# Causal attention layer of a decoder: float32r split products, reordered queues

## What is computed

```
h   = layernorm(x)                                # 16 batches of 128 rows x 256
qkv = h @ Wqkv.T                                  # 16 heads of 16
q   = q*cos + rotate_half(q)*sin ; k likewise
s   = einsum('bhqd,bhkd->bhqk', q, k) / 4 ; s[causal] = -inf
out = einsum('bhqk,bhkd->bhqd', softmax(s), v)
x   = x + out.reshape(...) @ Wout.T
```

## Time and profile before

| what | value |
|---|---|
| median of three runs | 1561.54 us (1561.36 to 1569.25) |
| the profiled execution, its span | 1564.6 us |
| TensorE busy | 1485.5 us, 95% |
| VectorE busy | 1068.3 us, 68% |
| ScalarE busy | 965.8 us, 62% |
| GpSimd busy | 727.0 us, 46% |
| mean granted TensorE clock | 0.983 |
| the causal block in it | from about 9 to 202 us |

### The profile page before, as it was taken

How to read it: one execution, slowest core, us unless ns; L and a number is a source line. 1 busy time by engine, 2 the same in 40 slices (tenths; PEclk the granted TensorE clock), 3 DMA queues, 4 the chain that set the end, 5 groups by cost and what they waited for, 6 DMA issues and landing times. The chain is left out here.

```text
span 1564.6 us, 30305 instructions
## 1 busy us (share of the span) xinstructions
PE 1485.5 (95%) x10256; PEld 1212.1 (77%) x10256; DVE 1068.3 (68%) x2475; ACT 965.8 (62%) x2612; POOL 727.0 (46%) x891
## 2 busy tenths in 40 slices
PE   5999979999999999899997999899999999989998
PEld 2666668888888888788874555489999999967887
DVE  4676657888888887655545777655566665588887
ACT  2667647777777777533325877577777777742222
POOL 3666625555555555233333433213444444447675
PEclk8999989999999999999997999999999999999999
DMA  6000020000000000000003000020000000000000
GB/s 246 2 1 1 2 97 5 3 5 3 5 3 4 3 3 2 22 1 1 1 5 130 2 2 1 15 92 8 8 8 8 1 8 5 1 1 14 11 15 17
DMA packets 15609, 29.82 MB, mean 19 GB/s; under 512 B 1505, under 2 KB 12002, under 8 KB 14690
## 3 DMA queue, kind: packets, MB, share of 16 engines
q1 hardware_dynamic: 15458, 27.89, 4.9%
HBM read 25.79 MB, written 2.10 MB: 18 GB/s over the span
## 5 line engine op out<-in xcount | busy, mean ns | idle before, releaser
L1453 POOL TENSOR_TENSOR weights_even<-weights_even,cross_reciprocal 128x512 f32<-128x512 f32 x64 | 66.6, 1041 | 201.9 <-DVE cross_reciprocal L1686 201.9
L934 POOL TENSOR_TENSOR cross_work<-cross_work,cross_reciprocal 128x512 f32<-128x512 f32 x64 | 66.6, 1040 | 174.6 <-DVE cross_reciprocal L1091 174.6
L1535 ACT ACTIVATE weights_even<-bank,cross_shift 128x128 f32<-128x128 f32 x256 | 90.5, 366 | 79.1 <-DVE cross_shift L1678 79.1
L1157 PE MATMUL bank<-ident,cross_work 128*128 128x128 f32 x768 | 117.6, 276 | 2.5 <-DVE cross_work L1069 2.2
L987 ACT ACTIVATE cross_work<-bank,cross_shift,cross_q_rms 128x128 f32<-128x128 f32 x256 | 113.6, 455 | 5.2 <-DVE cross_shift L1063 4.0
L1157 PEld LDWEIGHTS bank<-ident,cross_work 128*128 128x128 f32 x768 | 90.2, 141 | 30.0 <-DVE cross_work L1069 21.1
L2481 DVE TENSOR_REDUCE grouped_maxima<-bank 128x4 bf16<-128x512 f32 x128 | 82.3, 684 | 35.9 <-PE bank L2564 35.9
L1962 POOL TENSOR_TENSOR mlp_low_inner<-mlp_inner,mlp_high_inner 128x512 fp32r<-128x512 f32 x36 | 48.7, 1353 | 116.4 <-ACT mlp_high_inner L2005 116.4
L1676 DVE TENSOR_REDUCE cross_maxima<-bank 128x4 f32<-128x512 f32 x64 | 44.1, 690 | 84.6 <-PE bank L1818 84.6
L404 POOL TENSOR_TENSOR causal_masked_maxima<-causal_maxima,causal_constants 128x512 bf16<-128x512 bf16 x64 | 67.0, 1068 | 56.6 <-DVE causal_maxima L549 56.6
L2830 ACT ACTIVATE mx_silu<-bank 128x512 f32<-128x512 f32 x32 | 19.1, 598 | 113.4 <-PE bank L2980 113.3
(11 more groups left out here) (375 smaller groups left out, 5292.6 us busy)
## 6 DMA issues: line engine op xcount, KB each, us to landing
weights_even<-in_weights SPq DMA_DIRECT2D x2, 2560.0 KB, 11.8
weights_even<-in_weights SPq DMA_DIRECT2D x2, 1732.0 KB, 8.6
weights_odd_early<-in_weights SPq DMA_DIRECT2D x1, 3072.0 KB, 11.9
weights_odd_values<-in_weights SPq DMA_DIRECT2D x1, 3072.0 KB, 18.9
weights_odd_late<-in_weights SPq DMA_DIRECT2D x2, 1536.0 KB, 9.4
x<-in_x SPq DMA_DIRECT2D x4, 512.0 KB, 8.2
out<-mx_result SPq DMA_DIRECT2D x16, 128.0 KB, 1.7
weights_even<-in_weights SPq DMA_DIRECT2D x2, 512.0 KB, 5.8
```

The source lines that it names most:

```text
L934: pool.tensor_tensor(probs[x], probs[x], reciprocal[x][:, :].unsqueeze(2).to_broadcast([P, PER, P]), ALU.mult).then_inc(probs_divided, 1)
L1157: last = pe.transpose(bank[:, j * P:(j + 1) * P], source, core.ident[:, :])
L1453: pool.tensor_tensor(probs[x], probs[x], reciprocal[x][:, :].unsqueeze(2).to_broadcast([P, JOBS, P]), ALU.mult).then_inc(probs_divided, 1)
L1535: last = act.activation(probs[x][:, j, :], bank_scores[x][:, j * P:(j + 1) * P], ACT.Exp, scale=SCALE, bias=shift[x][:, j:j + 1], accum_ou ...
```

## The change

The four projections become three float32r products each. For that the block's own weights are split at its start, four pieces of 512 columns, by a ScalarE copy and a VectorE subtraction each. The two ScalarE copies of turned `h` and heads become one of up to 512 columns (`copy_turned`), followed by one VectorE subtraction of the same width (`low_turned`), which stands ahead of the maxima of pair 1; TensorE waits for it ahead of the value projection. The next block's weights are split by one ScalarE copy (`take_high`, last in the step) and one GpSimd subtraction a step later (`take_low`) in place of one VectorE and two GpSimd operations. On GpSimd the masked maxima of both pairs now stand ahead of that subtraction. VectorE normalises `h` one step earlier, behind the statistics, and takes the statistics of later chunks one step later. ScalarE's exponentials of pair 1 stand ahead of the mask of pair 1. TensorE subtracts the maxima of t pair 1 ahead of the scores of t+1 pair 0, those of t+1 pair 0 ahead of the scores of pair 1, and the transposed scores of pair 0 end the step that made them.

```
@@ scalar
+            act.wait_ge(core.weights_loaded[n], 16 * WEIGHT_PARTS)
+            for k in range(WEIGHT_JOBS):
+                columns = slice(512 * k, 512 * (k + 1))
+                act.activation(split[0][:, columns], raw[:, columns], ACT.Copy).then_inc(own_high, 1)
+            def copy_turned(t, s):
+                if batch_there(t + 2):
+                    act.wait_ge(layer.hT_filled, t + 3)
+                if batch_there(t - 2):
+                    act.wait_ge(headsT_filled, t - 1)
+                act.wait_ge(v_filled, min(nonneg(t + 1), BATCHES))
+                act.wait_ge(layer.y_filled, nonneg(t - 3))
+                act.activation(turned[s][0][:, turned_in(t)], bank_h[:, turned_in(t)], ACT.Copy)\
+                   .then_inc(turned_high, 1)
             def step(t, s):
-                    copy_hT(t + 2, s)
...
-                    copy_headsT(t - 2)
+                    copy_turned(t, s)
...
                     copy_keys_and_own_queries(t + 1, 1 - s)
+                if batch_there(t):
+                    exponentials(t, 1)
                 if batch_there(t + 1) and not begins(t + 1):
                     lay_mask(t + 1, 1)
                 if batch_there(t):
-                    exponentials(t, 1)
+                    take_high(t)
@@ vector
+            def low_turned(t, s):
+                dve.wait_ge(turned_high, turned_by(t))
+                dve.tensor_tensor(turned[s][1][:, turned_in(t)], bank_h[:, turned_in(t)],
+                                  turned[s][0][:, turned_in(t)].bitcast(F32), ALU.subtract).then_inc(turned_low, 1)
+            layer.dve_normalise(dve, 0)
+            for k in range(WEIGHT_JOBS):
+                dve.wait_ge(own_high, k + 1)
+                dve.tensor_tensor(split[1][:, columns], raw[:, columns], split[0][:, columns].bitcast(F32),
+                                  ALU.subtract).then_inc(own_low, 1)
             def step(t, s):
-                if batch_there(t + 2):
-                    layer.dve_normalise(dve, t + 2)
                 if batch_there(t + 1):
                     add_turned(t + 1)
+                if batch_there(t + 2) or batch_there(t - 2):
+                    low_turned(t, s)
                 if batch_there(t):
                     row_maxima(t, s, 1)
-                    take_high(t, s)
...
+                if batch_there(t + 3):
+                    if (t + 3) % CHUNK == 0:
+                        dve.wait_ge(chunk_statistics.rstd_ready, (t + 3) // CHUNK)
+                    layer.dve_normalise(dve, t + 3)
                 if batch_there(t + 2):
                     multiply_by_tables(t + 2)
@@ gpsimd
             def step(t, s):
                 if batch_there(t):
                     mask_maxima(t, s, 1)
-                if batch_there(t):
-                    split_weights(t, s)
                 if batch_there(t + 1):
                     mask_maxima(t + 1, 1 - s, 0)
+                if batch_there(t - 1):
+                    take_low(t - 1)
@@ tensor
+            def three_products(out, inputs, weights):
+                for c in range(EC):
+                    for x, y in PARTS:
+                        last = pe.matmul(out, inputs[x][:, c, :], weights[y][:, c, :],
+                                         start=(c == 0 and (x, y) == PARTS[0]),
+                                         stop=(c == EC - 1 and (x, y) == PARTS[-1]))
             def step(t, s):
-                if batch_there(t):
-                    scores_transposed(t, s, 0)
...
                     weigh_values(t - 1, 1 - s)
+                if batch_there(t + 2) or batch_there(t - 2):
+                    pe.wait_ge(turned_low, turned_by(t))
...
                     project_values(t + 1, 1 - s)
...
+                    project_heads(t - 2, s)
+                if batch_there(t):
+                    subtract_maxima(t, 1)
                 if batch_there(t + 1):
                     scores(t + 1, 1 - s, 0)
...
                 if batch_there(t + 1):
+                    subtract_maxima(t + 1, 0)
                     scores(t + 1, 1 - s, 1)
+                    scores_transposed(t + 1, 1 - s, 0)
```

More of the change, by code:

```diff
@@ L315, in place @@
             return part.rearrange(pattern, **sizes) if pattern else part
-        wqk = place(EC * 2 * EMBED, "p (c n) -> p c n", c=EC)
-        wv, wo = (place(EC * EMBED, "p (c n) -> p c n", c=EC) for k in range(2))
+        WEIGHT_JOBS = EC * 4 * EMBED // 512
+        raw = place(EC * 4 * EMBED)
+        split = [sbuf(f"{name}_weights", [P, EC * 4 * EMBED], F32R) for name in ("high", "low")]
+        wqk = [w[:, 0:EC * 2 * EMBED].rearrange("p (c n) -> p c n", c=EC) for w in split]
+        wv, wo = ([w[:, k * EC * EMBED:(k + 1) * EC * EMBED].rearrange("p (c n) -> p c n", c=EC) for w in split]
+                  for k in (2, 3))
         constants = sbuf("constants", [P, dram["causal_constants"].shape[1]])
@@ L325, in causal_attention @@
         qk_cos, qk_sin, qk = (place(2 * EMBED) for k in range(3))
-        hT = [layer.hT, place(EC * P, "p (c t) -> p c t", c=EC)]
+        turned = [[sbuf(f"{name}_turned{s}", [P, 2 * EMBED], F32R) for name in ("high", "low")] for s in range(2)]
+        hT = [[half[:, 0:EMBED].rearrange("p (c t) -> p c t", c=EC) for half in turned[s]] for s in range(2)]
+        headsT = [[half[:, EMBED:2 * EMBED].rearrange("p (c t) -> p c t", c=EC) for half in turned[s]]
+                  for s in range(2)]
         qT_bf = [sbuf(f"qT_bf{s}", [P, EC, P], BF16) for s in range(2)]
@@ L360, in chunk_at_end_of, with turned_in, turned_by @@
         def chunk_at_end_of(t):
-            return t + 3 if isinstance(t, int) and t + 3 in range(1, CHUNKS) else None
+            return t + 2 if t + 2 in range(1, CHUNKS) else None
         def begins(b):
             return isinstance(b, int) and b < 2
+        def turned_in(t):
+            return slice(0 if batch_there(t + 2) else EMBED, 2 * EMBED if batch_there(t - 2) else EMBED)
+        def turned_by(t):
+            return t + 3
         def slice_of(tensor, b):
@@ L432, in _ @@
         def _(act):
[L433 to L445, removed]
+            act.wait_ge(core.weights_loaded[n], 16 * WEIGHT_PARTS)
[11 more added lines that the diff above has]
+                   .then_inc(turned_high, 1)
+            qkT = bank_qkT.rearrange("p (x c t) -> p x c t", x=2, c=EC)
             def narrow_queries_and_own_keys(b, s):
@@ L671, in turn @@
                 last.then_inc(filled, 1)
-            def project_values(b, s):
-                pe.wait_ge(layer.hT_ready, b + 1)
-                for c in range(EC):
-                    last = pe.matmul(bank_h[:, 0:EMBED], hT[s][:, c, :], wv[:, c, :],
-                                     start=(c == 0), stop=(c == EC - 1))
-                last.then_inc(v_filled, 1)
-            def project_heads(b):
-                pe.wait_ge(headsT_ready, b + 1)
-                for c in range(EC):
-                    last = pe.matmul(bank_qk[:, 0:EMBED], headsT[:, c, :], wo[:, c, :],
-                                     start=(c == 0), stop=(c == EC - 1))
-                last.then_inc(layer.y_filled, 1)
+            def three_products(out, inputs, weights):
[4 more added lines that the diff above has]
+                                         stop=(c == EC - 1 and (x, y) == PARTS[-1]))
+                return last
@@ L687, in project_queries_and_keys, with project_heads @@
+            def project_values(b, s):
+                if b == 0:
+                    pe.wait_ge(own_low, WEIGHT_JOBS)
+                three_products(bank_h[:, 0:EMBED], hT[s], wv).then_inc(v_filled, 1)
+            def project_heads(b, s):
+                three_products(bank_qk[:, 0:EMBED], headsT[s], wo).then_inc(layer.y_filled, 1)
             def project_queries_and_keys(b, s):
-                pe.wait_ge(layer.hT_ready, b + 1)
+                pe.wait_ge(turned_low, turned_by(b - 2))
+                if b == 0:
+                    pe.wait_ge(own_low, WEIGHT_JOBS // 2)
@@ L689, in project_queries_and_keys @@
                 pe.wait_ge(qk_read, nonneg(b))
-                for c in range(EC):
-                    last = pe.matmul(bank_qk[:, :], hT[s][:, c, :], wqk[:, c, :], start=(c == 0), stop=(c == EC - 1))
-                last.then_inc(qk_filled, 1)
+                three_products(bank_qk[:, :], hT[s], wqk).then_inc(qk_filled, 1)
             def step(t, s):
-                if batch_there(t):
-                    scores_transposed(t, s, 0)
-                if batch_there(t):
-                    pe.wait_ge(v_ready, t + 1)
```

57 lines of the change are left out of this document (21 added, 36 removed).

## The result

The changed kernel takes **1571.48 us** (median of five runs, 1571.23 to 1576.34) against 1561.54: ratio 1.0052, 95% interval 1.0029 to 1.0076. Measured once more beside the experiments, twelve runs against 23 of the kernel before, it is 1570.52 against 1565.60: ratio **1.0044**, 1.0026 to 1.0062. So it is slower by some 7 us (1.0044 of 1565.6), between 4 and 10: the direction of the forecast, but about a third of its +19.5. Executions of one kernel spread by some 10 us (1560.61 to 1570.73 in those 23), in the profiles through the later layers, which the change doesn't touch; the causal block repeats within 0.3 us. What the edits do is therefore read from the block: by the start of its last update of `x`, 201.53 us before and 206.57 after. That difference, +5.04, is also the difference of the two profiled spans (1564.6 and 1569.6); the rest of the span is 1363.1 and 1363.0.

The account below looks back on a forecast made before the run. The prediction took TensorE's queue to set the 10.53 us step. Hand-over +6, start +1, tail +2.5 and clock +10 summed to +19.5 us on the median of 1561.54: 1581 us, range 1565 to 1594.

Parts of the forecast that it names:

- The products: TensorE's projections: query-key 1.48 us against 1.82, values 0.79 against 0.97, heads 0.71 against 0.95; saves 0.76 a step.
- The hand-over: Copy, subtraction, maxima, mask, exponentials: maxima 1.56 us later, TensorE waits 1.34 and 0.20; step 11.05 against 10.53, +6 us.
- the loop: Transposes of the heads, copy, subtraction, maxima, mask, exponentials, back to TensorE; makes a step 0.52 us longer.
- the clock: Steady steps: the new 1.54 us wait halves TensorE's clock in half of 12 steps, 6 x 1.7 = +10 us.
- rival 1: Steady steps: the wait is there but the clock holds; 1571 us, between 1566 and 1576; chance 0.22.
- `h` a step earlier: TensorE's wait for VectorE's normalised `h`, 0.2 to 0.27 us a step, goes.
- Start and tail: Start: splitting own weights delays the first projection, +1 us; tail: extra hop in steps 14 to 17, +2.5 us.
- The delayed addition: Start: next chunk's statistics (four reductions, 1.39 us) move to the end of the next step, delaying a later addition.
- Masks ahead of the weights: GpSimd's masks in the steps: hidden with 0.2 to 0.3 us to spare, costed at nothing.
- Rival 2: Steady steps: TensorE stays the bound and the products pay; step 9.5 us, kernel 1552.5; chance 0.10.

Follow-up runs that it names:

- Undoing the hop alone: Against the changed kernel, VectorE takes the maxima of the second half ahead of the subtraction of the turned halves; 1562.66 us, ratio 0.999 to the kernel before.
- the run with one product: Against the changed kernel, the four projections compute only high x high, leaving out both products with low halves; copies and subtractions stay; 1586.38 us.
- The run with 1.4 to 1.7 in one piece: Against the changed kernel, one ScalarE copy of the mask into a spare tile ahead of the first-half exponentials in twelve steps; 1593.65 us.
- the second profile: A second profile of the unaltered changed kernel; its last update of `x` starts at 206.65 us.
- `h` early: Against the changed kernel, VectorE normalises `h` behind the first maxima, ahead of the update of `x`; 1567.56 us.
- three pieces (1.67 us): Against the changed kernel, two VectorE operations of 128x256 into a spare tile ahead of the division of the heads in twelve steps; 1577.69 us.
- the three edits: Against the changed kernel: second-half maxima ahead of the turned halves' subtraction, `h` ahead of the update of `x`, scores ahead of the subtracted maxima; 1557.73 us.

## Why the prediction was wrong in size

**The products** held: query-key 1.50 us (122.50 to 124.00) against 1.48, values and heads together about 1.53 against 1.50. The Trainium skill, FP8 and Floating Point Precision, section Matmul Precision, says that true float32 takes four passes through the array; three of four would be an estimated 1.37. The trace here doesn't agree (1.50, which is 0.82 of the 1.82), and the starts of the earlier trace rows were the better price.

**The hand-over** held as far as the exponentials. Counted from the transposes at 115.30 the copy starts at 1.07, the subtraction at 1.70, the maxima at 2.31, the mask at 3.62, the exponentials at 4.68: each 0.36 to 0.39 behind the forecast, by the 0.35 us that the heads are late. The subtraction of the maxima starts at 5.31 (forecast 4.95), the output's transposes at 8.70 (8.58), and the step is 10.97 (11.05). Undoing the hop alone gave 0.72 us back; that cause is shown. That 10.97 comes so near 11.05 is partly luck. From the subtraction to the next transposes TensorE took 5.66 and not 6.10: scores and transposed scores, now next to each other, start together (121.43 and 121.44) and took 1.07 where the prediction added 0.33 and 1.06. And the prediction closed the loop through the query-key projection and TensorE's unchanged work, while the run with one product kept its step at full clock with that projection 0.93 shorter; the loop closes through VectorE.

**The step that failed is the clock**: "I take half: 6 x 1.7 = +10". There was no fall. Its size rested on a wait of 1.34 + 0.20 that stood in for the 1.55 of the earlier trace rows. The sum of the idle time was nearly right, 1.28 against 1.54, but not its place: TensorE was held up by the heads and by query and key in the transposes (0.64 by the value projection), and came to the subtraction 0.84 later than forecast, when the exponentials were only 0.36 later. 1.34 + 0.36 - 0.84 is the 0.86 in the timeline. The run with 1.4 to 1.7 in one piece does show the clock falling in half of the steps, but "half" was a mean between none and all that no row gave, so that agreement is luck; the price of a fall was 0.9 there, half of the forecast's. Without the term the sum is 1571, rival 1, which held 0.22 of the chance.

**Why the waits came apart: `h` a step earlier**, which the prediction cost at nothing. It named what is late next, but did not ask what stands behind `h` on VectorE. In its new place `h` takes 0.71 us and not 0.40, with tables and heads queued behind it, and VectorE is on the loop. With `h` taken out of there TensorE starts the value projection 2.25 us behind the transposes of `h` (103.98 - 101.73) and not 2.75 (118.05 - 115.30): that is 0.50 of the 0.84, and the wait is 1.04. The other 0.34 stays with `h` moved, and no run took it apart. Getting it and the scores out of there, on top of the maxima's, took the step from 10.25 to 9.79; of these edits alone, the scores gave 0.52 and `h` 0.33.

**Start and tail.** The start forecast at +1 came out at -1.6 and, in the second profile, at -0.2. The two waits of 1.55 for `h` are gone, which the prediction had not counted as a gain; between 25 and 50 us no wait of TensorE is now over 1.10. The delayed addition that it named behind the moved statistics did come, three times, with waits of 0.76, 1.10 and 1.92 us, and the third took the clock with it; TensorE's wait and the window behind it:

```profile
50.62 1.12 PE L691 MATMUL bank<-ident,weights_even 128*128 128x128 f32 x4 [1.92 <-DVE weights_even L555]
```

```profile
50.00:53.00 3.00, 2.38 (x32) 1.93 (x36) 2.36 (x4) 1.17 (x4) 2.53 (x3) 0.50 0.00 0
```

That the gain at the start comes from the lost waits is read from the traces and was not tried; the two profiles part at that fall, where the clock stays low for 3.4 us in this one and for 6.8 in the second. The tail came at +2.2 against +2.5, but at +0.9 in the second profile, so that its nearness is luck. **Masks ahead of the weights** cost nothing, as forecast, and shown by the run without them.

**Rival 2** (faster at a step of 9.5) named its condition rightly: maxima and mask 1.5 us earlier. Taking the maxima first gives back the hop of the copy and the subtraction, and with `h` and the scores moved as well the step of 9.79 comes near its 9.5.

Left open: what decides whether a wait takes the clock. In the steady steps waits of 1.02 to 1.04 us took it once in nine (`h` early), those of 1.38 to 1.40 each of six times and those of 1.5 to 1.7 in the same run never, those of 2.05 to 2.35 seven times in eleven. Open too is what the float32r products would give without any hand-over in front of the maxima, which wasn't tried.

## What to carry to other kernels

When an engine that is 95% busy gets less to do, ask at once which latency loop is next, and write that loop down over all engines, with what is queued in front of each hand-over; here putting one 0.69 us subtraction behind the maxima instead of ahead of them was worth 0.72 us a step. Where a new hand-over must be added, put it behind whatever releases another engine. And place a wait before costing its effect on the clock: about the same idle time cost nothing in three pieces (1.67 us) and some 0.9 us every second step in one (1.4 to 1.7).

## What the runs showed of the hardware

Normalising `h`, one VectorE operation from SBUF to SBUF, has no fixed price. Its durations (least/median/most ns, first and last start) in the kernel before, after, and with the three edits:

```profile
L144 DVE TENSOR_SCALAR causal_h<-x,mean,rstd x16: 402/404/625, 8.9 to 167.1; 128x256 f32<-128x256 f32 x16
```

```profile
L144 DVE TENSOR_SCALAR causal_h<-x,mean,rstd x16: 401/713/756, 8.9 to 168.1; 128x256 f32<-128x256 f32 x16
```

```profile
L144 DVE TENSOR_SCALAR causal_h<-x,mean,rstd x16: 405/1156/1158, 8.8 to 154.7; 128x256 f32<-128x256 f32 x16
```

In the first it runs while GpSimd has nothing to do (GpSimd sat idle for 3.83 us ahead of 116.17). In the others it starts beside GpSimd's masked maxima and ends just behind one of them: in the timeline of after at 124.88, the masks at 124.73; with the three edits it begins with the second of the row's two masks, and takes that mask's whole time and 0.15 more:

```profile
114.47 2.04 POOL L418 TENSOR_TENSOR causal_masked_maxima<-causal_maxima,causal_constants 128x512 bf16<-128x512 bf16 x2 [2.21 <-DVE causal_maxima L563]
115.50 1.16 DVE L144 TENSOR_SCALAR causal_h<-x,mean,rstd 128x256 f32<-128x256 f32 x1
```

The Trainium skill, SBUF — State Buffer, section Who interferes with whom, says that VectorE and GpSimd share a port pair as an exclusive lock, and that a `tensor_scalar` can be among the operations that need it. The trace agrees in that `h` ends just behind the mask, with 0.31 to 0.75 us more for it here.

The other surprise is that taking two thirds of the projections' work away made the kernel slower, in one run of it: the block ends 12.9 us later (219.45 against 206.57). The loop did not get shorter (10.98 at full clock), TensorE's wait in it grew into one long piece, and the clock fell.
